# A graph kernel's first layer: leaky sums moved to VectorE, half the logit products, another order of selections, window loads and node-tile loads

## The reference

```python
xl = (x @ Wl).reshape(n, H, C)            # n = 50000, H = 4 heads of C = 32
xr = (x @ Wr).reshape(n, H, C)
m = xl[src] + xr[dst]                     # an edge from src to dst, and one from each node to itself
e = jax.nn.leaky_relu(m, 0.2)
logits = jnp.einsum('ehc,hc->eh', e, att)
amax = jax.ops.segment_max(logits, dst, num_segments=n)
ex = jnp.exp(logits - amax[dst])
alpha = ex / (jax.ops.segment_sum(ex, dst, num_segments=n)[dst] + 1e-16)
out = jax.ops.segment_sum(alpha[:, :, None] * xl[src], dst, num_segments=n)
# then bias, normalisation over all nodes, elu, x + ..., layernorm, and the second network
```

## Time and profile before

| what | value |
|---|---|
| median of the runs shown | 3507.84 us |
| the profiled execution, its own time | 3512.0 us |
| its span, first to last instruction | 3510.2 us |
| granted TensorE clock, mean over the span | 0.959 |
| busy over the span: PE, DVE, ACT, POOL | 3011.9, 2482.2, 1716.1, 1647.1 us |
| the node sums of DVE in the own stage (L1768), first and last start | 58.6 and 455.5 us |
| the copies of ACT in the edge stage (L1241), first and last start | 473.6 and 1157.0 us |

### The profile page before, as it was taken

One profiled execution on the slowest core, in us unless ns is written; L12 is line 12 of the kernel. 1 busy time (PEld: TensorE's weight loads), 2 busy tenths in 40 slices (PEclk: granted clock), 3 DMA queues, 4 the chain that ended last, 5 costly groups with the idle time before them and its releaser, 6 DMA issues.

```text
span 3510.2 us, 68649 instructions
## 1 busy us (share of the span) xinstructions
PE 3011.9 (86%) x17947; PEld 2215.3 (63%) x17947; DVE 2482.2 (71%) x7956; ACT 1716.1 (49%) x4046; POOL 1647.1 (47%) x2010
## 2 busy tenths in 40 slices
PE   4666679999999588879979999979998999996997
PEld 3666668888888455458865555547884555555665
DVE  5666646666666588878867777764446777776998
ACT  2333323333333244449985666644444666664665
POOL 0000055555555022227767777741227777763555
PEclk9999989999999799999999999999999999998999
DMA  5666667777777388869963333338983333337997
GB/s 129 192 183 189 189 154 165 167 168 165 165 166 162 90 244 237 240 202 293 293 230 94 105 103 104 104 86 273 301 287 100 103 103 103 104 98 242 343 330 262
DMA packets 804343, 637.66 MB, mean 182 GB/s; under 512 B 81661, under 2 KB 682066, under 8 KB 803954
## 3 DMA queue, kind: packets, MB, share of 16 engines
q1 hardware_dynamic: 599874, 396.49, 39.8%
q0 software_dynamic: 54208, 130.20, 13.9%
q10 hardware_dynamic: 149872, 106.57, 10.1%
HBM read 398.80 MB, written 234.13 MB: 180 GB/s over the span
## 4 chain that ended last, share of the span: by engine, by line
PE 28%; POOL 22%; issue 12%; DVE 12%; DMA 11%; ACT 9%; ACTq 3%; SPq 2%; DVEq 0%; POOLq 0%
POOL work L900 22%; DMA work<-in_x_dram 5%; PE bank L981 4%; ACT work L1371 4%; PE bank L978 3%; DMA work<-w_d 3%; PE bank L1179 3%; PE bank L1186 3%; PE bank L991 3%; PE bank L992 3%; PE bank L967 2%; PE bank L966 2%; ACT work L1363 1%; ACTq L463 1%; DVE seg_max L1726 1%
## 5 line engine op out<-in xcount | busy, mean ns | idle before, releaser
L2023 DVE SCALAR_TENSOR_TENSOR work<-bank,coef,work 128x128 f32<-128x128 f32 x2400 | 674.0, 342 | 245.2 <-ACT work L1405 241.8
L1132 PE MATMUL bank<-basis_s,work 128*128 128x512 f32 x1600 | 756.0, 595 | 1.5 <-ACT work L1398 1.5
L858 POOL DMA_INDIRECT work<-xl_d,slot_src x400 | 382.4, 956 | 740.5 <-issue 540.7
L900 POOL DMA_INDIRECT work<-x_d,slot_src x400 | 384.1, 960 | 126.3 <-issue 121.6
L900 POOL DMA_INDIRECT work<-h_d,slot_src x400 | 385.1, 963 | 123.8 <-issue 121.6
L1405 ACT ACTIVATE work<-bank,coef 128x128 f32<-128x128 f32 x800 | 293.9, 367 | 224.7 <-PE bank L1132 224.7
L1132 PEld LDWEIGHTS bank<-basis_s,work 128*128 128x128 f32 x1600 | 274.3, 191 | 196.6 <-issue 192.6
L1143 PEld LDWEIGHTS bank<-work 128*126 128x126 f32 x1600 | 206.9, 189 | 101.6 <-issue 100.9
L1186 PEld LDWEIGHTS bank<-work 128*128 128x128 f32 x1552 | 205.8, 193 | 97.7 <-issue 92.8
L1179 PE MATMUL bank<-work,loop_s 128*128 128x512 f32 x392 | 212.8, 625 | 28.0 <-ACT work L1445 26.7
L872 POOL DMA_DIRECT2D conv_d<-work x99 | 73.8, 750 | 335.5 <-DVE work L1912 325.1
(11 more groups left out here) (278 smaller groups left out, 6895.5 us busy)
## 6 DMA issues: line engine op xcount, KB each, us to landing
w_d<-work SPq DMA_DIRECT2D x800, 62.5 KB
work<-in_x_dram SPq DMA_DIRECT2D x194, 256.0 KB, 4.2
work<-x_d SPq DMA_DIRECT2D x194, 256.0 KB, 4.6
w_d<-work SPq DMA_DIRECT2D x400, 66.9 KB
work<-w_d SPq DMA_DIRECT2D x398, 64.0 KB, 3.4
work<-w_d ACTq DMA_DIRECT2D x390, 64.0 KB, 3.5
xl_d<-work SPq DMA_DIRECT2D x97, 256.0 KB, 2.5
xr_d<-work SPq DMA_DIRECT2D x97, 256.0 KB, 3.1
```

The source lines that it names most:

```text
L858: pool.indirect_dma_start(gathered(i)[:, c, :], None, xl_d, bass.IndirectOffsetOnAxis(ap=slot_src[:, a:a + 1], axis=0)).then_inc(e_in[i % ...
L900: pool.indirect_dma_start(quad(0, i % 3)[:, c, :], None, (x1_d, h1_d)[l], bass.IndirectOffsetOnAxis(ap=slot_src[:, a:a + 1], axis=0)).then ...
L1132: pe.matmul(psum[YBANKS[k % 5]][:, :], quad(1, i % 2)[:, c, :], basis_s[:, l, :, :].rearrange("k b n -> k (b n)"), start=True, stop=True). ...
L2023: ins = dve.scalar_tensor_tensor(o, psum[YBANKS[k % 5]][:, b * D:(b + 1) * D], coef[:, i, l, c, b:b + 1], o, ALU.mult, ALU.add)
```

## The change

In the edge stage ACT writes m once, as it is (`edges_mixed`). A new function `leaky(i)` on DVE makes max(0.2 m, m) out of it, and `logits(i)` multiplies that alone: 4 matmuls. DVE's order becomes `turn_matrix(i + 2)`, `maxima(i)`, `leaky(i + 1)`, `values(i)`, `slot_matrix(i + 1)`, and `hot_types(i)` last. Of a row's 8 windows SP loads 2 and ACT 6. ACT reads the 6 starts of row i + 3 and issues its first 3 windows at the end of its turn i (behind `weigh(i)`); the last 3 of a row i + 2 it issues in turn i, right behind `edges_mixed(i + 1)`. In the own stage SP issues `load_own(q + 3)` ahead of `save_own(q)`.

```diff
@@ -62,6 +62,7 @@
 TILES_E = CHAINS * ROWS
 GAP = 256
 SLOTS = TE + 1
+ON_SP = 2
 HALF = (TE + 1) // 2
 WINDOW = 112
 HALVES = ((0, HALF), (HALF, TE))
@@ -296,7 +297,7 @@
             [sem(f"ew_out{c}") for c in range(CHAINS)])
         xr_out, window_in, nodes_ready = (
             [sem(f"xr_out{k}") for k in range(3)], [sem(f"window_in{k}") for k in range(3)], sem("nodes_ready"))
-        mx_ps, pt_ok, m_cp = sem("mx_ps"), sem("pt_ok"), sem("m_cp")
+        mx_ps, pt_ok, m_cp, lr_ok = sem("mx_ps"), sem("pt_ok"), sem("m_cp"), sem("lr_ok")
         lg_ps, arg_ok, tb_ps, ex_ok, v_ok, es_ok, ec_ps, ec_cp = (
             sem("lg_ps"), sem("arg_ok"), sem("tb_ps"), sem("ex_ok"), sem("v_ok"), sem("es_ok"),
             sem("ec_ps"), sem("ec_cp"))
@@ -444,15 +445,18 @@
         def turned_pick(i):
             return quad(9, i % 3)[0:WINDOW, :, 0:TE]
 
-        def load_windows(eng, h, i):
+        def window_starts(eng, i, first, last):
 
             if i >= 3:
                 eng.wait_ge(mx_ps, i - 2)
-            row = base_at[i:i + 1, h * CHAINS:(h + 1) * CHAINS]
-            starts = nc.values_load_multi_w_load_instructions(
-                row, engines=[eng.engine], min_val=0, max_val=N + EPAD - WINDOW,
+            return nc.values_load_multi_w_load_instructions(
+                base_at[i:i + 1, first:last], engines=[eng.engine], min_val=0, max_val=N + EPAD - WINDOW,
                 skip_runtime_bounds_check_because="a window lies before the last node, or in the rows set out edge by edge")[1]
-            for c, at in enumerate(starts):
+
+        def load_windows(eng, i, first, starts):
+
+            for k, at in enumerate(starts, first):
+                h, c = divmod(k, CHAINS)
                 eng.dma_start(window(h, i)[0:WINDOW, c, :], xr_d[bass.ds(at, WINDOW), :]).then_inc(window_in[i % 3], 16)
 
         def load_packed(eng, l, q, first, last):
@@ -649,21 +653,21 @@
             sp.wait_ge(pos_ok, 2)
             sp.dma_start(rel_d, rel_bf[:, :, :].rearrange("i c e -> i (c e)")).then_inc(drop_out, 16)
             for q in range(QUADS):
-                save_own(q)
                 if q + 3 < QUADS:
                     load_own(q + 3)
+                save_own(q)
             sp.wait_ge(zero_ok, 1)
             end = addresses(sp, end_at[0:1, 0:1])[0]
             sp.dma_start(w_d[0][bass.ds(end, P), :], work[15][:, 0:WIDE]).then_inc(zero_out, 16)
             sp.wait_ge(nodes_ready, 1)
             sp.wait_ge(drop_out, 16 * H + 16)
             for i in range(3):
-                load_windows(sp, 0, i)
+                load_windows(sp, i, 0, window_starts(sp, i, 0, ON_SP))
                 if i < 2:
                     load_block(i)
             for i in range(ROWS + 2):
                 if i + 3 < ROWS:
-                    load_windows(sp, 0, i + 3)
+                    load_windows(sp, i + 3, 0, window_starts(sp, i + 3, 0, ON_SP))
                 if i % BLOCK == 0 and BLOCK <= i < ROWS - BLOCK:
                     load_block(i // BLOCK + 1)
                 if i >= 2:
@@ -983,13 +987,12 @@
                 last.then_inc(mx_ps, 1)
 
             def logits(i):
-                pe.wait_ge(m_cp, i + 1)
+                pe.wait_ge(lr_ok, i + 1)
                 pe.wait_ge(heads_ok, 1)
                 if i:
                     pe.wait_ge(ex_ok, i)
                 for c in range(CHAINS):
-                    pe.matmul(logit_t, att_heads[:, c, :], quad(8, i % 2)[:, c, :], start=c == 0, stop=False)
-                    last = pe.matmul(logit_t, att_heads[:, c, :], quad(14, i % 2)[:, c, :], start=False, stop=c == CHAINS - 1)
+                    last = pe.matmul(logit_t, att_heads[:, c, :], quad(14, i % 2)[:, c, :], start=c == 0, stop=c == CHAINS - 1)
                 last.then_inc(lg_ps, 1)
 
             def turn_back(i):
@@ -1237,9 +1240,8 @@
             def edges_mixed(i):
                 act.wait_ge(mx_ps, i + 1)
                 if i >= 2:
-                    act.wait_ge(lg_ps, i - 1)
-                act.activation(flat(8, i % 2), psum[i % 2][:, :], ACT.Relu, scale=1.0 - SLOPE)
-                act.activation(flat(14, i % 2), psum[i % 2][:, :], ACT.Copy, scale=SLOPE).then_inc(m_cp, 1)
+                    act.wait_ge(lr_ok, i - 1)
+                act.activation(flat(8, i % 2), psum[i % 2][:, :], ACT.Copy).then_inc(m_cp, 1)
 
             def gains(i):
                 act.wait_ge(tb_ps, i + 1)
@@ -1278,19 +1280,23 @@
                 own_projected(q)
             act.wait_ge(pos_ok, 2)
             act.wait_ge(nodes_ready, 1)
-            for i in range(3):
-                load_windows(act, 1, i)
+            split = ON_SP + (2 * CHAINS - ON_SP) // 2
+            for i in range(2):
+                load_windows(act, i, ON_SP, window_starts(act, i, ON_SP, 2 * CHAINS))
             edges_mixed(0)
-            for i in range(ROWS + 1):
-                if i + 1 < ROWS:
+            for i in range(-1, ROWS + 1):
+                if i >= 0 and i + 1 < ROWS:
                     edges_mixed(i + 1)
-                if i + 3 < ROWS:
-                    load_windows(act, 1, i + 3)
-                if i:
+                if i >= 0 and i + 2 < ROWS:
+                    load_windows(act, i + 2, split, starts[split - ON_SP:])
+                if i >= 1:
                     compacted(i - 1)
-                if i < ROWS:
+                if 0 <= i < ROWS:
                     gains(i)
                     weigh(i)
+                if i + 3 < ROWS:
+                    starts = window_starts(act, i + 3, ON_SP, 2 * CHAINS)
+                    load_windows(act, i + 3, ON_SP, starts[0:split - ON_SP])
             for k in range(CHAINS - 1):
                 act.wait_ge(join_arg, k + 1)
                 act.activation(join[:, 4:6, :], join[:, 2:4, :], ACT.Exp).then_inc(join_exp, 1)
@@ -1709,6 +1715,12 @@
                 dve.tensor_scalar(turned_pick(i), row.rearrange("p (c e) -> p c e", c=CHAINS), lane_p[0:WINDOW, 0:1], None,
                                   ALU.is_equal).then_inc(pt_ok, 1)
 
+            def leaky(i):
+                dve.wait_ge(m_cp, i + 1)
+                if i >= 2:
+                    dve.wait_ge(lg_ps, i - 1)
+                dve.scalar_tensor_tensor(flat(14, i % 2), flat(8, i % 2), SLOPE, flat(8, i % 2), ALU.mult, ALU.max).then_inc(lr_ok, 1)
+
             def maxima(i):
 
                 k, b = i % 2, i // BLOCK
@@ -1772,15 +1784,18 @@
             slot_matrix(0)
             turn_matrix(0)
             turn_matrix(1)
+            leaky(0)
             for i in range(ROWS):
-                if i % 4 == 0:
-                    hot_types(i)
-                maxima(i)
                 if i + 2 < ROWS:
                     turn_matrix(i + 2)
+                maxima(i)
+                if i + 1 < ROWS:
+                    leaky(i + 1)
                 values(i)
                 if i + 1 < ROWS:
                     slot_matrix(i + 1)
+                if i % 4 == 0:
+                    hot_types(i)
 
             dve.wait_ge(ec_cp, ROWS)
             dve.wait_ge(tile_in, 16 * 4)
```

## The result

The changed kernel takes 3578.1 us (median of 4 runs, 3573.1 to 3585.84), the kernel before 3512.2 us on the same chip. The ratio is 1.0192, with a 95% interval of 1.0150 to 1.0233: slower by about 66 us, where I had forecast 48 us faster. The profiled execution took 3585.84 us, its span is 3584.0 us, and its mean granted clock 0.911.

What follows compares the result with a forecast made beforehand. It took SP's load-behind-store loop to bound the own stage and PE's own order the edge stage. From 3512.0 us, less 98 (own stage), plus 50 (late windows), came 3464, or 3460 as a median; 8-in-10 range 3378 to 3545.

Steps and rivals of the forecast that it cites:

- The own stage: Own stage: with the load ahead of the stores a quad takes 3.08 us instead of 4.09, gaining 98 us.
- The loop of the windows: Edge stage, one edges_mixed to the next: 4.23 us plus the landing, 7.4 us a row, PE waiting in every row.
- the same landing of 3.15 us: Edge stage: time from the start of ACT's third late window issue to its landing, taken between 2.4 and 3.6 us.
- the mix, taken at 2.90 us: Edge stage, last term of the loop: PE's mix until ACT sees it finished, 2.90 us as in a profiled plain row.
- the price of the edge stage: Edge stage: a row goes from 6.90 to 7.4 us, costing 50 us; bounds -27 and +92 us.
- a clock well below 1.0 as a sign that I was wrong: Edge stage, changed profile: a clock well below 1.0 at PE's mix would show the forecast wrong.
- my average wait of 1.8 us: Edge stage: PE's new wait per plain row before the mix, 1.8 us, put beneath the wait that lowers the clock.
- TensorE's clock falls in the wait: Edge stage rival: longer waits lower PE's clock, a row takes 8.5 us, 3568 us in all; chance 0.14.
- ScalarE's load I under-sized: Edge stage: ACT busy 5.3 us a row with six window issues and reading of starts at 0.82 us.
- at most 0.2 us for `hot_types`: Edge stage: `hot_types` last in DVE's order delays one row in four by some 0.2 us at most.
- PE's own path: Edge stage: PE's own work per row falls from 6.90 to 5.8 us with four logit matmuls and a wait gone.
- a row of 6.4 us: Edge stage: estimate by the skill's lone-DMA figure, 2.1 us a window, making the stage 50 us faster; the forecast rejected it.

Runs made afterwards that it cites:

- e1: The kernel before with one edit, SP issuing the load of a quad of x ahead of the stores: 3392.3 us, 0.9679 of before.
- e3: The changed kernel with eight filler products a row on PE, unread, ahead of the next mix: 3472.3 us, 0.9919 of before.
- e2: The kernel before with only the windows split and issued late as in the change, eight logit products kept: 3691.3 us, 1.0523 of before.
- e4: The changed kernel with ScalarE's windows issued a row earlier, all for row i + 3, starts read a row ahead: 3416.3 us, 0.9749 of before.
- e7: The kernel of e4 with ScalarE's reading of the starts moved behind its first three window issues: 3420.6 us, 0.9749 of before.
- e10: The kernel of e7 with SP's reading of the next starts moved ahead of its stores of sums: 3409.0 us, 0.9716 of before.
- e11: As e10, with three windows on SP and five on ScalarE: 3386.3 us, 0.9669 of before.
- e5: The changed kernel with the windows as in the kernel before, four on each queue: 3346.8 us, 0.9540 of before.
- e9: The kernel of e5 with SP and ScalarE reading their next starts right behind their window issues: 3349.9 us, 0.9559 of before.
- e8: The kernel of e2 with four filler products a row on PE: 3606.5 us, 1.0289 of before.

## Why the prediction was wrong

**The own stage was right, and a little short.** I forecast 3.08 us a quad and 98 us; it is 2.89 us, DVE's own time, and 116 us (112 in e1). The DMA engines hold a share of 0.94 without becoming the bound.

**The loop of the windows was the right one, and its average came out partly by luck.** I named the wait of L982 for the windows as what decides, and it is there: 1.4 us a row, forecast 1.5. Over the 55 rows in 600 to 1100 us that the trace shows from copy to copy, the mix starts 4.67 us behind the copy on average, forecast 4.5. But I had the same landing of 3.15 us and a wait in every row. The runs show landings of 2.3 to 5.7 us where a window ends the wait, and some 40% of the rows without a wait.

**The term that failed is the mix, taken at 2.90 us, and with it the price of the edge stage.** I forecast 7.4 us a row, +50 us; it was 8.85, +193 us. In the same 55 rows the mix takes 4.14 us on average, from 2.89 to 5.42, until ScalarE sees it: 1.24 us a row above its term, 123 us of the 143 that are missing. In e3, where only the clock and PE's filling differ, it takes 2.87 us, and the row is 1.15 us shorter, 113 us. So most of the miss is the granted clock: 0.78 on average, with mixes at the lower level of 1.2 GHz behind the waits. PE's work shows it as a whole: 412 us in 56.5 rows is 7.3 us a row, and in e3, without the fillers, (478 - 131) / 64.9 = 5.4 us. The part of this that lies in the logits and in compact comes ahead of the mix and takes up some of the wait. The remaining 0.3 us of a row between 7.4 and e3's 7.71 are, at least partly, the fillers themselves in the weigh rows. I had named a clock well below 1.0 as a sign that I was wrong, and that sign came.

**Why I thought that the clock would hold.** The row at 207.40 had full speed behind 1.93 us of idle time, the one at 216.46 had not behind 3.50. I compared my average wait of 1.8 us with these two numbers. Two things were wrong in that. The waits are not all average: 3.67 us in the row shown above, 2.93 in e2. And the two numbers don't carry over from stage to stage: the wait of 1.98 us at 709.42 is as short as the one at 207.40, yet the lower level follows within the mix, while the products behind 207.40 keep the full clock (0.39 us a pair to 209.46). Ahead of 207.40 PE ran dense products; ahead of 709.42 it ran two transposes of 16 columns, behind 0.29 us of waiting, and eight light instructions of 32 columns (L1027). That this work ahead is what makes the difference is my reading; no run changed it by itself. The fillers show the coupling by the dose: 0.78, 0.90 and 1.00 with none, four and eight.

**The rival had it.** The slower case, "TensorE's clock falls in the wait", gave 3568 us; measured were 3578. I gave it 0.14, and let only half of it into the range, whose end of 3545 the result passed. Its condition, landings of 3.6 us or more, was met where it counts: 13 of the 15 landings that the chain names were longer. A spread of landings was enough; they need not all be late.

**The products that were saved are part of the harm, not its cause.** Taking four products away lengthens PE's wait by what they took. Still e2, which keeps all eight, loses as much: 8.92 us a row. The lateness alone is sufficient.

**ScalarE's load I under-sized.** I counted 5.3 us a row with the reading at 0.82 us. The reading of six starts took 1.39 us in the changed kernel (median). Behind the late windows this was hidden; e4, e7, e10 and e11 show it as the next bound. The leaky sums and DVE's new order can't be priced from these runs: e5 gains 45 us with them and with half the products, but PE's waits for the maxima became longer in it, where I had forecast at most 0.2 us for `hot_types`.

The Trainium skill ("DMA: Bandwidth & Descriptors", Anatomy of one DMA) led to a row of 6.4 us by its fixed 2.0 us for a lone DMA. The runs decide against that use of it. In e2's timeline above ScalarE's last issue ends at 701.39, and the mix that waits for the windows starts at 705.80, 4.4 us later; no version with late windows came near 6.4 us a row on average.

**What stays open.** Why e5 takes 6.46 us a row where PE's own path is some 5.8, and why six windows on ScalarE cost 0.8 us a row even when they are early. In both the clock is below 1.00 again (0.94 and 0.86), so part of it will be this same coupling, but no run here took it apart. A store of sums on SP waits until the store of the row before has landed. The chain of work through e5's 600 to 1000 us lies in such landings for 34.4% of the time, and e9's names none in the shares that it lists, yet e9's rows are as long. So SP's stores look like one of at least two paths of nearly the same length; that isn't shown by a run. In e7 ten waits for windows are left, up to 1.9 us.

## What to carry to other kernels

When a load is moved, count how many uses of other buffers lie between its issue and its own use, for each half of it separately: here a split that balanced two queues put half of one queue's loads one row too late. Price a new wait on TensorE twice, once as time and once as clock, and by its spread, not by its average: here 1.4 us a row was made of waits up to 5.0 us, products behind the long ones ran at half speed, and the clock nearly doubled the price (187 us in e2, some 100 in e8, where fillers held it). A wait that left the clock alone in one stage (1.93 us) did not in another (1.98 us). A few useless products in the wait are a quick test of that, and a late load that is moved earlier is the cure (3347 us in place of 3472).

## What the runs showed of the hardware

Reading a few integers from on-chip memory into registers is not cheap, and its price does not grow evenly with their number. In the same table, the least in 600 to 1000 us: four starts took 0.31 us on ScalarE and 0.47 on SP (e5), two 0.64 on SP (the change), three 0.86 on SP and five 1.13 on ScalarE (e11), six 1.33 on ScalarE (e7). The four were read as one aligned half of the table's row, and no run read four at another place, so the count and the place are not told apart. The lines of e11, 600 to 1000 us, three starts on SP and five on ScalarE:

```profile
L450 ACTq TENSOR_LOAD <-base_at x59: 1127/1179/3280, 599.0 to 997.5; - x59
L450 SPq TENSOR_LOAD <-base_at x58: 862/891/1883, 606.3 to 998.5; - x58
```

The reading of six took up to 4.2 us in e4, where it stands beside SP's stores of sums, and 3.1 us at the most in e7. That the stores slow it is supported by these two places alone.

A window of 56 KB took 2.3 to 5.7 us from the start of its issue to its landing where it ended a wait of the changed kernel, at a DMA share of 0.57.
